# Expert tiles: SiLU on the gate half alone, the place read after the transpositions, TensorE's tile loop written out

## The chip, the core and the metric

The kernel runs on one core of a Trainium2 chip. Each of the core's engines follows its own instruction stream and meets the others through semaphores: TensorE (PE, with its weight loads shown apart as PEld), VectorE (DVE), ScalarE (ACT), GpSimd (POOL), and SyncE (SP), which issues DMAs. The metric is the device time of one execution in microseconds (us), lower is better. An engine's sequencer is the part that reads its instructions, computes addresses in registers, waits for semaphores and hands work on to the engine; in the profile its own instructions carry a q (PEldq for TensorE's).

## The reference, cut to what matters

Two transformer layers run one after the other on 4096 tokens of 256 channels; the change touches only the last block, a mixture of experts with a shared expert beside it:

```python
def _L1_ffn_ref(x, Wr, Wg, Wu, Wd, Sg, Su, Sd):      # 8 experts, hidden size 512
    xt = x.reshape(T, H)                              # T = 4096, H = 256
    scores = softmax(xt @ Wr)
    topk_w, topk_idx = top_k(scores, 2)
    topk_w = topk_w / (topk_w.sum(-1, keepdims=True) + EPS)
    g = silu(einsum('th,ehd->etd', xt, Wg))
    u = einsum('th,ehd->etd', xt, Wu)
    out_all = einsum('etd,edh->eth', g * u, Wd)
    out = sum(out_all[topk_idx, tok] * topk_w[..., None], axis=1)
    return out + silu(x @ Sg) * (x @ Su) @ Sd
```

## The kernel before

After routing, the tokens are sorted by expert and cut into NE = 71 tiles of 128 rows. Tile i is worked off by five engines at once, each with its own function of the same name `tile`, and what sets the order is the order in which each engine's code is written, with semaphores between them.

On TensorE, `tile(i, h)` does four things in this order. First `h_transpose_e(i - 1, ...)` transposes the hidden rows `hb` of the tile before (4 matmuls with the identity, L2260). Then `gate_up_e(i, ...)` multiplies the tile's tokens with the expert's gate matrix into PSUM bank 2 (w = 0) and its up matrix into bank 3 (w = 1): each product of 32-bit numbers is three matmuls of high and low parts (L1857 to L1859, the helper `three`), so 6 matmuls for the gate half and 6 for the up half. Then `x_transpose_e(i + 1, ...)` transposes the next tile's tokens (2 matmuls, L2244), and `down_e(i - 1, ...)` multiplies the transposed hidden rows of the tile before with the down matrix (12 matmuls, again L1857 to L1859, with `heh` and `hel` as operands).

Where an expert's weights lie in SBUF is known only at run time. `place_of(i)` (L2272) reads one number from the table `of_tile` in SBUF into a register of TensorE's sequencer and computes expert and address from it:

```python
def place_of(i):
    return pe.value_load(of_tile[0:1, bass.ds(i, 1)], min_val=0, max_val=SLOTS * E - 1)
```

In a looped pair of tiles the first one reads two places, its own and that of the tile before; the second one gets the latter from the first as a register and reads one. Tiles 0 to 4 and 67 to 70 are written out; tiles 5 to 66 run in `pe.Fori(2, (NE - 5) // 2)`, 31 turns of two tiles (L2312).

The other engines, per tile: ACT turns the transposed hidden rows into their high part `heh` (`h_high_e`, L789), then `silu_e(i)` computes SiLU of bank 2 into `gs` (L784), then `x_high_e(i + 1)` makes `xeh` (L779) and issues the load of a later tile's tokens. DVE makes the low part `hel` (`h_low_e`, L1798), then `hidden_e(i)` multiplies bank 3 with `gs` into `hb` (L1794), then `x_low_e(i + 1)` makes `xel` (L1788), then `y_out(i - 1)` copies the output to `ye` (L1806). SP stores `ye`. POOL gathers tokens, loads the experts' weights and splits them into high and low parts.

The semaphores that matter: `e_gu` (gate and up of a tile done), `e_si` (SiLU done), `e_hb` (hidden rows done), `e_ht` (transposed), `e_hlo` (`hel` done), `e_xlo` (`xel` done), `e_dn` (down done), `w_ready` (an expert's weights split). The transposition waits for `e_hb` of the tile before, and `gate_up_e` for `e_xlo`, `w_ready` and the same `e_hb`.

Of the kernel before, what the change touches and what calls it, by code (L numbers as in the profile page):

```python
# [40 lines left out]
E = 8  # L41
EH = 512
EW = 2 * KD * EH + EH // P * D
SLOT = 2 * EW
NE = 2 * NT + E - 1
# [22 lines left out]
def wait(eng, sem, n):  # L68

    if not isinstance(n, int) or n > 0:  # L70
        eng.wait_ge(sem, n)
# [22 lines left out]
def build(nc, cst, xT, x, wqkvgT, wave_cols, bias_cols, coupling_rows, woutT, bout, wgu_rows, wd_rows, wqk_T, wo_rows, bo, wr, experts, out):  # L94
    ctx = ExitStack()
    with ctx:
# [311 lines left out]
        def _(act):  # L408
# [366 lines left out]

            def x_high_e(i, h):
                act.wait_ge(e_t, i + 1)
                wait(act, e_gu, i - 1)
                act.activation(xeh[:, h].rearrange("p a c -> p (a c)"), PS[:, h, 0:D], ACT.Copy).then_inc(e_xhi, 1)  # L779

            def silu_e(i, h):
                act.wait_ge(e_gu, i + 1)
                wait(act, e_hb, i - 1)
                act.activation(gs[:, h], PS[:, 2], ACT.Silu).then_inc(e_si, 1)  # L784

# [9 lines left out]
            def tile(i, h, groups=None, first=False, final=False):  # L795
                if not first:
                    h_high_e(i - 1, 1 - h)
                silu_e(i, h)
                if not final:
                    x_high_e(i + 1, 1 - h)  # L800
                    if not isinstance(i, int) or DIRECT <= i + 3 < NE:
                        if groups is not None:
                            act.wait_ge(d_rows, 16 * groups)
                        rows(i + 3, 1 - h)

            x_high_e(0, 0)
            tile(0, 0, first=True)
            for i in range(1, 5):
# [18 lines left out]
            at = 4 * (NCH - 1) + 2  # L827
# [249 lines left out]
        def _(dve):  # L1077
# [62 lines left out]
            for cos_, _, turns in TABLES:  # L1140
                dve.tensor_scalar(cos_[:].bitcast(U32), turns[:].bitcast(U32), 0x7FFFFFFF, None, ALU.bitwise_and).then_inc(turns_done, 1)
# [647 lines left out]
                                  xeh[:, h].rearrange("p a c -> p (a c)").bitcast(F32), ALU.subtract).then_inc(e_xlo, 1)  # L1789

            def hidden_e(i, h):
                dve.wait_ge(e_si, i + 1)
                wait(dve, e_ht, i - 1)
                dve.tensor_tensor(hb[:, h], PS[:, 3], gs[:, h], ALU.mult).then_inc(e_hb, 1)  # L1794
# [13 lines left out]
            def tile(i, h, first=False, final=False):  # L1808
                if not first:
                    h_low_e(i - 1, 1 - h)  # L1810
                hidden_e(i, h)
                if not final:
                    x_low_e(i + 1, 1 - h)
                if not first:
                    y_out(i - 1, 1 - h)
# [34 lines left out]
            at = 4 * last + 3  # L1850
# [3 lines left out]
        def _(pe):  # L1854
            def three(out_, wh, wl, vh, vl, first, last_):

                pe.matmul(out_, wh, vh, start=first, stop=False)  # L1857
                pe.matmul(out_, wh, vl, start=False, stop=False)  # L1858
                return pe.matmul(out_, wl, vh, start=False, stop=last_)  # L1859
# [375 lines left out]
            def x_transpose_e(i, h):  # L2235
                rows = xe[:, h]
                if isinstance(i, int) and i < DIRECT:
                    pe.wait_ge((d_row0, d_row1)[h], 16 * (i // 2 + 1))
                    rows = xe[:, i] if i < 2 else xd[:, i - 2]
                else:  # L2240
                    pe.wait_ge(d_xe[h], 8 * (i - h) - 8 * (DIRECT - 2))
                wait(pe, e_xlo, i - 1)
                for k in range(KD):
                    t = pe.transpose(PS[:, h, k * P:(k + 1) * P], rows[:, k * P:(k + 1) * P], ident)  # L2244
                t.then_inc(e_t, 1)

            def gate_up_e(i, h, base_):
                pe.wait_ge(e_xlo, i + 1)
                wait(pe, e_hb, i)
                for w in range(2):  # L2250
                    for k in range(KD):
                        at, lo = (bass.ds(base_ + i * EW + (w * KD + k) * EH, EH) for i in range(2))
                        mm = three(PS[:, 2 + w], xeh[:, h, k], xel[:, h, k], EWs[:, at], EWs[:, lo], k == 0, k == KD - 1)
                mm.then_inc(e_gu, 1)

            def h_transpose_e(i, h):
                pe.wait_ge(e_hb, i + 1)
                wait(pe, e_hlo, i - 1)
                for j in range(4):
                    t = pe.transpose(PS[:, 4 + h, j * P:(j + 1) * P], hb[:, h, j * P:(j + 1) * P], ident)  # L2260
                t.then_inc(e_ht, 1)

            def down_e(i, h, base_):
                pe.wait_ge(e_hlo, i + 1)
                wait(pe, e_y, i - 1)
                for j in range(4):
                    at, lo = (bass.ds(base_ + i * EW + 2 * KD * EH + j * D, D) for i in range(2))
                    mm = three(PS[:, 6 + h, 0:D], heh[:, h, j], hel[:, h, j], EWs[:, at], EWs[:, lo], j == 0, j == 3)
                mm.then_inc(e_dn, 1)

            def place_of(i):
                return pe.value_load(of_tile[0:1, bass.ds(i, 1)], min_val=0, max_val=SLOTS * E - 1)  # L2272

            def tile(i, h, before=None, first=False, final=False):
                place = place_of(i)
                expert, at = place % E, place // E * SLOT
                if not first:
                    if before is None:
                        before = place_of(i - 1)
                        before = before // E * SLOT  # L2280
                    h_transpose_e(i - 1, 1 - h)
                pe.wait_ge(w_ready, expert + 1)
                gate_up_e(i, h, at)
                if not final:
                    x_transpose_e(i + 1, 1 - h)
                if not first:
                    down_e(i - 1, 1 - h, before)
                return at

# [14 lines left out]
            x_transpose_e(0, 0)  # L2304
            down_wide(1, 3)
            at = tile(0, 0, first=True)
            pe.wait_ge(d_add, 2 * AHEAD)
            at = tile(1, 1, at)
            at = tile(2, 0, at)
            at = tile(3, 1, at)  # L2310
            tile(4, 0, at)
            with pe.Fori(2, (NE - 5) // 2) as r:  # L2312
                at = tile(2 * r + 1, 1)
                tile(2 * r + 2, 0, at)
            at = tile(NE - 4, 1)
            for i in range(NE - 3, NE):
                at = tile(i, i % 2, at, final=i == NE - 1)
            h_transpose_e(NE - 1, 0)
            pe.wait_ge(d_xlo, AHEAD + 1)
# [92 lines left out]
```

## Time and profile before

| what | us |
|---|---|
| median of 3 runs | 1096.64 (1096.44 to 1098.18) |
| the profiled execution's own time | 1101.61 |
| its span, first to last instruction | 1099.7 |
| PE busy | 1032.2 (94%) |
| DVE busy | 764.7 (70%) |
| ACT busy | 489.6 (45%) |
| POOL busy | 442.0 (40%) |

The profiled execution took 1.91 us more than its span, and 4.97 us more than the median. Starts are in us from the span's start. A group of instructions has a line, an engine, an operation, what it writes and reads, a count, its busy time and the mean of one in ns; a bracket behind a timeline row tells how long the engine was idle before it and what ended that. "issue" means that the engine waited for nothing that the profile shows, so for its own sequencer or for something unseen. The experts' tiles lie between 611 and 982 us.

### The profile page before, as it was taken

What the parts mean: (1) busy time and instruction counts of PE and PEld (TensorE: products, weight loads), DVE (VectorE), ACT (ScalarE), POOL (GpSimd) and SP (SyncE); (2) the same over time, 40 slices, a digit from 0 to 9 for tenths busy, and PEclk for the clock granted to TensorE, in tenths of its full rate; (3) what the DMA queues carried; (4) which work ended last, traced back from release to release, by engine and by line L of the source; (5) the groups of instructions that cost most, each with busy time, mean ns of one, the idle gap of its engine ahead of it and who ended that gap; (6) DMA issues with size and microseconds to landing.
All of it is one profiled execution on the core that took longest, in us unless ns stands there. A gap on an engine that the chain in (4) does not pass through costs nothing.

```text
span 1099.7 us, 19315 instructions
## 1 busy us (share of the span) xinstructions
PE 1032.2 (94%) x5960; PEld 901.9 (82%) x5961; DVE 764.7 (70%) x1290; ACT 489.6 (45%) x914; POOL 442.0 (40%) x445
## 2 busy tenths in 40 slices
PE   6898997799999999999999999989999999999994
PEld 5676776799999998999988787878888888888883
DVE  7988998899999987787878343333444444347886
ACT  6745755774344444666751222222322222233326
POOL 1000201555544446322100787975633200018886
PEclk9999998999999999999999999999999999999997
DMA  8100000010000000311250557464413111213335
GB/s 315 70 32 20 1 29 1 1 35 1 0 0 0 0 1 1 120 40 39 64 205 6 187 172 242 141 183 160 156 52 107 56 48 54 70 58 108 123 106 191
DMA packets 41350, 87.83 MB, mean 80 GB/s; under 512 B 5970, under 2 KB 27732, under 8 KB 39892
## 3 DMA queue, kind: packets, MB, share of 16 engines
q0 software_dynamic: 9696, 35.66, 10.5%
q1 hardware_dynamic: 20804, 39.20, 10.0%
q10 hardware_dynamic: 10800, 12.32, 3.6%
q8 instruction: 29, 0.48, 0.2%
q14 instruction: 21, 0.17, 0.0%
HBM read 57.80 MB, written 29.36 MB: 79 GB/s over the span
## 4 chain that ended last, share of the span: by engine, by line
PE 53%; DVE 19%; DVEq 10%; POOL 8%; issue 5%; ACT 4%; DMA 1%; ACTq 0%; POOLq 0%
PE PS L1857 14%; PE PS L1859 13%; PE PS L1858 13%; POOL gathered L1043 6%; PE PS L2260 3%; PE PS L2012 2%; DVEq L1433 2%; DVEq L1280 2%; POOL pause L1047 1%; DVEq L1447 1%; PE PS L2244 1%; DVE hx L1292 1%; PE PS L1910 1%; DVEq L1293 1%; DVE qinv L1283 1%
## 5 line engine op out<-in xcount | busy, mean ns | idle before, releaser
L1794 DVE TENSOR_TENSOR hb<-PS,gs 128x512 f32<-128x512 f32 x71 | 49.1, 692 | 154.0 <-ACT gs L784 143.4
L1043 POOL DMA_INDIRECT gathered<-expert_outputs,pos x64 | 66.7, 1043 | 139.5 <-DMA expert_outputs<-ye 127.2
L1857 PE MATMUL PS<-EWs,xeh 128*128 x284 | 119.8, 422 | 0.0
L784 ACT ACTIVATE gs<-PS 128x512 f32<-128x512 f32 x71 | 42.5, 598 | 162.3 <-PE PS L1859 154.0
L1859 PE MATMUL PS<-EWs,xel 128*128 x284 | 112.5, 396 | 0.0
L1858 PE MATMUL PS<-EWs,xeh 128*128 x284 | 111.8, 394 | 0.0
L1857 PE MATMUL PS<-WGh,bxh 128*128 128x352 f32 x256 | 88.0, 344 | 13.4 <-DVE hv L1427 10.5
L2012 PE MATMUL PS<-WD,htf 128*128 128x256 f32 x384 | 88.5, 380 | 1.6 <-ACT htf L573 1.5
L1857 PE MATMUL PS<-EWs,heh 128*128 x284 | 85.7, 302 | 3.9 <-issue 3.9
L789 ACT ACTIVATE heh<-PS 128x512 fp32r<-128x512 f32 x71 | 42.5, 598 | 104.4 <-PE PS L2260 86.9
L1798 DVE TENSOR_TENSOR hel<-PS,heh 128x512 fp32r<-128x512 f32 x71 | 49.1, 691 | 55.0 <-ACT heh L789 46.3
L1858 PE MATMUL PS<-WGl,bxh 128*128 128x352 f32 x256 | 85.3, 333 | 0.0
L1859 PE MATMUL PS<-WGh,bxl 128*128 128x352 f32 x256 | 85.2, 333 | 0.0
L2012 PEld LDWEIGHTS PS<-WD,htf 128*128 128x128 f32 x384 | 71.2, 190 | 10.9 <-ACT htf L573 2.5
L1858 PE MATMUL PS<-EWs,heh 128*128 x284 | 80.1, 282 | 0.0
L1859 PE MATMUL PS<-EWs,hel 128*128 x284 | 80.0, 282 | 0.0
L865 POOL TENSOR_TENSOR bq<-bx,qsc 128x512 f32<-128x512 f32 x16 | 19.6, 1226 | 117.9 <-DVE bx L1294 117.9
L1857 PEld LDWEIGHTS PS<-EWs,xeh 128*128 128x128 f32 x284 | 53.9, 190 | 16.0 <-issue 0.6
L1857 PEld LDWEIGHTS PS<-WGh,bxh 128*128 128x128 f32 x256 | 50.2, 196 | 17.2 <-issue 11.9
L1859 PEld LDWEIGHTS PS<-EWs,xel 128*128 128x128 f32 x284 | 53.7, 189 | 10.5
L1858 PEld LDWEIGHTS PS<-EWs,xeh 128*128 128x128 f32 x284 | 53.9, 190 | 9.4
L1857 PEld LDWEIGHTS PS<-EWs,heh 128*128 128x128 f32 x284 | 53.5, 188 | 4.7 <-issue 4.6
(387 smaller groups left out, 3013.5 us busy)
## 6 DMA issues: line engine op xcount, KB each, us to landing
raw_of<-experts POOLq DMA_DIRECT2D x6, 1536.0 KB
expert_outputs<-ye SPq DMA_DIRECT2D x71, 128.0 KB
xe<-tokens_by_expert ACTq DMA_DIRECT2D x65, 128.0 KB
xraw<-xT SPq DMA_DIRECT2D x8, 512.0 KB, 4.1
X<-x SPq DMA_DIRECT2D x1, 4096.0 KB, 13.3
tokens<-X SPq DMA_DIRECT2D x8, 512.0 KB, 3.1
y<-X SPq DMA_DIRECT2D x7, 512.0 KB
raw_of<-experts SPq DMA_DIRECT2D x2, 1536.0 KB, 9.5
```

The source lines that it names most:

```text
L784: act.activation(gs[:, h], PS[:, 2], ACT.Silu).then_inc(e_si, 1)
L789: act.activation(heh[:, h].rearrange("p a c -> p (a c)"), PS[:, 4 + h], ACT.Copy).then_inc(e_hhi, 1)
L1043: pool.indirect_dma_start(out=gathered[c][:, j, t], out_offset=None, in_=YS, in_offset=bass.IndirectOffsetOnAxis(ap=pos[:, j, 4 * c + t:4 ...
L1280: dve.drain()
L1433: dve.drain()
L1794: dve.tensor_tensor(hb[:, h], PS[:, 3], gs[:, h], ALU.mult).then_inc(e_hb, 1)
L1798: dve.tensor_tensor(hel[:, h].rearrange("p a c -> p (a c)"), PS[:, 4 + h], heh[:, h].rearrange("p a c -> p (a c)").bitcast(F32), ALU.subtr ...
L1857: pe.matmul(out_, wh, vh, start=first, stop=False)
L1858: pe.matmul(out_, wh, vl, start=False, stop=False)
L1859: return pe.matmul(out_, wl, vh, start=False, stop=last_)
L2012: mm = pe.matmul(PS[:, 7, i * D:(i + 1) * D], htf[:, i, k], WD[:, k], start=k == 0, stop=k == FT - 1)
L2260: t = pe.transpose(PS[:, 4 + h, j * P:(j + 1) * P], hb[:, h, j * P:(j + 1) * P], ident)
```

## The change

Three edits. (1) TensorE signals `e_gu` after the gate half and again after the up half. ACT's SiLU waits for the first of the two signals, and DVE's product now waits itself for the second one as well as for the SiLU. (2) In TensorE's `tile`, the transposition comes first and the read of the place follows it. (3) TensorE's loop is gone: tiles 5 to 66 are written out, and each passes its place on to the next, so every tile reads one. The loops of ACT, DVE and SP stay.

```diff
             def x_high_e(i, h):
                 act.wait_ge(e_t, i + 1)
-                wait(act, e_gu, i - 1)
+                wait(act, e_gu, 2 * i - 2)
...
             def silu_e(i, h):
-                act.wait_ge(e_gu, i + 1)
+                act.wait_ge(e_gu, 2 * i + 1)
                 wait(act, e_hb, i - 1)
...
             def hidden_e(i, h):
+                dve.wait_ge(e_gu, 2 * i + 2)
                 dve.wait_ge(e_si, i + 1)
...
                         mm = three(PS[:, 2 + w], xeh[:, h, k], xel[:, h, k], EWs[:, at], EWs[:, lo], k == 0, k == KD - 1)
-                mm.then_inc(e_gu, 1)
+                    mm.then_inc(e_gu, 1)
...
             def tile(i, h, before=None, first=False, final=False):
+                if not first:
+                    h_transpose_e(i - 1, 1 - h)
                 place = place_of(i)
                 expert, at = place % E, place // E * SLOT
-                if not first:
-                    if before is None:
-                        before = place_of(i - 1)
-                        before = before // E * SLOT
-                    h_transpose_e(i - 1, 1 - h)
                 pe.wait_ge(w_ready, expert + 1)
                 gate_up_e(i, h, at)
                 if not final:
                     x_transpose_e(i + 1, 1 - h)
                 if not first:
+                    if before is None:
+                        before = place_of(i - 1)
+                        before = before // E * SLOT
                     down_e(i - 1, 1 - h, before)
                 return at
...
-            tile(4, 0, at)
-            with pe.Fori(2, (NE - 5) // 2) as r:
-                at = tile(2 * r + 1, 1)
-                tile(2 * r + 2, 0, at)
-            at = tile(NE - 4, 1)
-            for i in range(NE - 3, NE):
+            at = tile(4, 0, at)
+            for i in range(5, NE):
                 at = tile(i, i % 2, at, final=i == NE - 1)
```

On TensorE, this is where one looped turn begins in the kernel before. `hb` are the hidden rows, `of_tile` the table of places; "ISA" and "REGISTER_ALU" are the sequencer's own steps, and the matmul at L2260 is the first of the transpositions:

```order
L2272 TENSOR_LOAD of_tile
L2272 ISA x3
L2272 TENSOR_LOAD of_tile
L2272 ISA x2
L71 REGISTER_ALU [waits d_ehb]
L2260 MATMUL PS<-C,hb 128x128 [waits d_ehlo]
L2260 MATMUL PS<-C,hb 128x128 x3
L2282 ISA
L2248 REGISTER_ALU [waits d_wready]
L1857 ISA [waits d_ehb,d_exlo]
L1857 MATMUL PS<-EWs,xeh 128x512
```

And this is the same place, between two tiles, in the changed kernel, whose lines from L1794 on count one more:

```order
L1860 MATMUL PS<-EWs,hel 128x256
L2261 MATMUL PS<-C,hb 128x128 [waits d_ehlo,d_ehb]
L2261 MATMUL PS<-C,hb 128x128 x3
L2273 TENSOR_LOAD of_tile
L2273 ISA x2
L2280 ISA
L1858 ISA [waits d_ehb,d_exlo,d_wready]
L1858 MATMUL PS<-EWs,xeh 128x512
```

Both reads stood ahead of the transposition and its wait for `e_hb`; now one read stands between the transposition and the first gate matmul.

On DVE, around the product `hb` of a looped tile, `hel`, `xel` and `ye` being the low parts and the output copy, the kernel before has:

```order
L1798 TENSOR_TENSOR hel<-PS,heh 128x512 [waits d_ehhi]
L1794 TENSOR_TENSOR hb<-PS,gs 128x512 [waits d_eht,d_esi]
L1787 REGISTER_ALU
L1788 TENSOR_TENSOR xel<-PS,xeh 128x256 [waits d_exhi]
L1806 COPY ye<-PS 128x256 [waits d_est1,d_edn]
```

and the changed kernel:

```order
L1799 TENSOR_TENSOR hel<-PS,heh 128x512 [waits d_ehhi]
L1792 ISA
L1795 TENSOR_TENSOR hb<-PS,gs 128x512 [waits d_eht,d_esi,d_egu]
L1787 REGISTER_ALU
L1788 TENSOR_TENSOR xel<-PS,xeh 128x256 [waits d_exhi]
L1807 COPY ye<-PS 128x256 [waits d_est1,d_edn]
```

The order of DVE's work is the same; the product has one wait more and one register step ahead of it.

## Rows read from the trace of the kernel before

**Rows 1.** The page, busy time and share of the span.

```profile
PE 1032.2 (94%) x5960; PEld 901.9 (82%) x5961; DVE 764.7 (70%) x1290; ACT 489.6 (45%) x914; POOL 442.0 (40%) x445
```

**Rows 2.** Busy time by stretch: start:end, us, engines (count), clock, DMA share, GB/s.

```profile
632.00:742.00 110.00, 102.47 (x587) 86.74 (x587) 42.71 (x80) 29.09 (x60) 90.59 (x93) 0.97 0.62 185
742.00:953.00 211.00, 211.00 (x1253) 181.72 (x1252) 88.18 (x166) 61.20 (x125) 57.14 (x15) 1.00 0.27 89
953.00:978.00 25.00, 25.00 (x152) 21.79 (x151) 11.79 (x23) 8.03 (x15) 0.00 (x0) 1.00 0.13 42
```

**Rows 3.** Timeline of PE: start, us; transpositions of tiles 5, 25, 67 and last.

```profile
633.03 0.65 PE L2260 MATMUL PS<-C,hb 128*128 128x128 f32 x4
...
745.87 0.65 PE L2260 MATMUL PS<-C,hb 128*128 128x128 f32 x4
...
958.06 0.60 PE L2260 MATMUL PS<-C,hb 128*128 128x128 f32 x4
...
977.88 0.66 PE L2260 MATMUL PS<-C,hb 128*128 128x128 f32 x4
```

**Rows 4.** Timeline of one written-out tile, from its first gate matmul.

```profile
968.46 0.49 PE L1857 MATMUL PS<-EWs,xeh 128*128 x1
968.80 0.39 PE L1858 MATMUL PS<-EWs,xeh 128*128 x1
...
969.72 0.39 PE L1859 MATMUL PS<-EWs,xel 128*128 x1
...
971.09 0.39 PE L1859 MATMUL PS<-EWs,xel 128*128 x1
...
971.52 0.60 ACT L784 ACTIVATE gs<-PS 128x512 f32<-128x512 f32 x1 [2.27 <-PE PS L1859]
...
972.14 0.69 DVE L1794 TENSOR_TENSOR hb<-PS,gs 128x512 f32<-128x512 f32 x1 [1.78 <-ACT gs L784]
...
972.75 0.41 DVE L1788 TENSOR_TENSOR xel<-PS,xeh 128x256 fp32r<-128x256 f32 x1
972.84 0.28 PE L1859 MATMUL PS<-EWs,hel 128*128 x1
972.96 0.60 PE L2260 MATMUL PS<-C,hb 128*128 128x128 f32 x4
...
973.42 0.49 PE L1857 MATMUL PS<-EWs,xeh 128*128 x1
```

**Rows 5.** Sequencer's steps by line: ns min/median/max, first and last start.

```profile
L2272 PEldq TENSOR_LOAD <-of_tile x1: 300/300/300, 971.4 to 971.4; - x1
...
L2272 PEldq SEQ_ASSERT  x1: 18/18/18, 972.0 to 972.0; - x1
L2282 PEldq FUSED_REGOPS  x1: 76/76/76, 972.9 to 972.9; - x1
L2312 PEldq COMPARE_BRANCH  x21: 222/222/222, 743.4 to 946.1; - x21
```

**Rows 6.** The same for the reads of 684 to 686.8 and of 632 to 742.

```profile
L2272 PEldq TENSOR_LOAD <-of_tile x2: 299/602/904, 684.5 to 685.9; - x2
...
L2272 PEldq TENSOR_LOAD <-of_tile x29: 297/305/918, 632.2 to 738.5; - x29
```

**Rows 7.** Timeline, and who PE waited for (us, times, longest).

```profile
686.63 0.65 PE L2260 MATMUL PS<-C,hb 128*128 128x128 f32 x4 [1.88 <-issue]
...
735.91 0.60 ACT L789 ACTIVATE heh<-PS 128x512 fp32r<-128x512 f32 x1 [5.75 <-remote]
...
737.43 0.38 PE L1857 MATMUL PS<-EWs,heh 128*128 x1 [2.92 <-issue]
...
PE PS L2260 <- issue: 4.5, 6, 1.9
```

**Rows 8.** Instruction fetches in 440 to 600 and 600 to 980: packets, MB, share.

```profile
q8 instruction: 9, 0.15, 0.4%
...
q8 instruction: 4, 0.07, 0.1%
```

## The prediction

> **What bounds the kernel now.** The page first: PE is busy 94% of the span and no other engine over 70% [rows 1], so what counts is what PE does and what delays it. Then the stretches [rows 2]: from 742 to 953 us PE's busy time is the whole 211.00 of 211.00. Busy does not mean at its peak, since PE's durations overlap, so the third view is the pace: the starts of the transpositions. Tiles 25 to 67 took (958.06 - 745.87) / 42 = 5.05 us each, and these are looped tiles; the four written out behind the loop took (977.88 - 958.06) / 4 = 4.955 us each [rows 3]. Same matmuls, 0.1 us less. Tiles 5 to 25 took (745.87 - 633.03) / 20 = 5.64 us each [rows 3]; there the DMAs are at 0.62 against 0.27, the clock at a mean of 0.97 and PE busy only 102.47 of 110 us [rows 2].
>
> The fourth view is one written-out tile [rows 4]. Call the start of its first gate matmul G = 968.46. The last gate matmul starts at G + 1.26 (969.72), the last up matmul at G + 2.63, SiLU at G + 3.06, the product `hb` at G + 3.68, and `hb` ends at G + 4.37. The last down matmul starts at G + 4.38, the transposition at G + 4.50 and the next gate matmul at G + 4.96. So two chains end together: PE's own queue, and last up matmul, SiLU, `hb`, transposition. A third is just behind: `xel` waits on DVE for `hb` and ends at G + 4.70, and the next gate matmul needs it. And the second gate matmul comes 0.34 us after the first, where the others stand (971.09 - 968.80) / 10 = 0.229 us apart: TensorE's sequencer is 0.1 us late there.
>
> Fifth, the sequencer. Its read begins at 971.4 and is done at 972.0 [rows 5], while PE still works on the matmuls queued before; then nothing happens in the sequencer until `hb` is done (972.14 + 0.69 = 972.83), and its next step (L2282) starts at 972.9 [rows 4, 5]. So a wait for a semaphore stops the sequencer, while matmuls already handed on run.
>
> **The change part by part.** *The loop goes.* A turn has a branch (0.22 us, rows 5) and a second read (0.6 us with its register steps, rows 5) ahead of the first tile's transposition. Most of it hides behind the queue, but the measured difference between a looped and a written-out tile is 5.052 - 4.955 = 0.097 us. For 62 looped tiles: 6.0 us.
>
> *The early SiLU.* It can start at G + 1.26 + 0.43 = G + 1.69, if PE's last matmul and ACT's start stand as far apart as now (971.09 to 971.52, rows 4), and ends at G + 2.29. Then `hb` waits for the up half alone: G + 2.63 + 0.43 = G + 3.06, plus the additional wait in DVE's sequencer. No row shows that; the nearest steps, 18 to 76 ns each [rows 5], bound it by 0 and 0.15, and I take 0.08. So `hb` runs from G + 3.14 to G + 3.83, 0.54 us earlier, and `xel` ends well before it is needed. Alone this would bring nearly nothing at the transposition, since PE's own queue holds it at G + 4.50; what it frees is the sequencer, at about G + 3.89.
>
> *The read behind the transposition.* From there the sequencer hands on the transpositions, reads the place (0.6 + 0.05 us) and needs what it needs now from the transposition's release to the first gate matmul: 972.9 to 973.42, 0.52 us, of which some 0.1 is the wait for `xel` (ends 973.16), which goes. That gives G + 3.89 + 0.65 + 0.42 = G + 4.96. The bounds are 0.1 us below (no additional wait in DVE, 4.88) and 0.1 us above (the wait for `xel` was not what took the time, 5.05). PE's own work gives 0.46 + 12 x 0.229 + 0.23 + 12 x 0.117 = 4.84 if the sequencer is never late, and 4.95 with its lateness. So I take 4.95 us a tile: the room that the early SiLU makes (0.54 us) is used up by the read (0.65 us) that is moved into it, and the written-out pace of now remains. Queued behind the moved read on TensorE are the expert's wait (`w_ready`) and all of gate and up; nobody else waits for it. SP's and POOL's queues are passed by nothing.
>
> *The DMA-heavy stretch.* 20 tiles at 5.05 would be 101.0 us; they took 112.84 [rows 3], so 11.8 us are irregular. One kind is at the loop's turns: PE waited 4.5 us in 6 pieces just ahead of a transposition for nothing that the profile shows, the longest 1.88 us at 686.63 [rows 7]. In that piece stand both reads of a turn, one of them taking 904 ns instead of 300 [rows 6]. The mean clock of 0.97 over 110 us [rows 2] is 0.03 x 110 / 0.5 = 6.6 us at the lower level of 1.2 GHz; it fell after the two longest idle times of PE, this one and the next, so each cost half of 3.3 us, some 1.6 us, beside itself. So reads explain about 6.1 us. The other kind is at 734 to 746: `heh` waited 5.75 us for a signal of work that PE had long done, and PE then 2.92 us [rows 7]; with the half clock behind it this one cost some 4.7 us. The profiled execution is 4.97 us above the median, so I take this to be of that execution alone; that is argued, not shown. The rest, 1.0 us, I leave.
>
> With the change a turn's second read is gone, but each read is now where nothing covers it: a slow one costs up to 0.6 us in full. Of 29 reads from 632 to 742 the median is 305 ns and the longest 918 [rows 6]; I allow 2.1 us (five of 20 reads slow by 0.4 us).
>
> *Instruction fetch.* Written out, TensorE's stream is longer. In 440 to 600 us, where PE's code has no loop, the queue q8, TensorE's by its rest while TensorE loops, fetched 9 times, once per 17.8 us, and the share of 0.4% of 16 engines in 160 us is about 1.1 us each; from 600 to 980 it was 4 [rows 8]. So about 325 / 17.8 = 18 fetches come in. PE was not left waiting for any of the nine, so I cost them at nothing; their cover is the code already fetched, and without it they cost 18 x 1.1 = 20 us.
>
> Here a rule of the Trainium skill bears on the case. The page Runtime: NRT & Kernel Launch, section Instruction fetch mechanics, says that a taken branch whose target is outside the window of fetched code forces a fetch and stalls. By that rule 31 turns would each hold a fetch, and writing out would bring far more than 6 us. The trace does not agree that it happens here: the branch took 222 ns in all 21 turns from 743 to 946 and fetches were only 4 in 380 us [rows 5, 8]; the sum goes without it.
>
> **The sum.** In the profiled execution tiles 5 to 67 took 325.0 us [rows 3]. After: 62 x 4.95 = 306.9, plus 2.1 = 309.0. Against its own time: 1101.6 - 16.0 = 1085.6. Against the median, which I take to be without the 4.7 us: 320.3 - 309.0 = 11.3, so 1096.6 - 11.3 = 1085.3. What comes behind the tiles (the shared expert on PE, the gather on POOL) starts from their end and moves with it. POOL isn't late: it is busy 57 of 211 us [rows 2].
>
> **The rivals.**
>
> 1. *The sequencer gets ahead.* If the next step after the wait is quicker than I count, the pace is PE's own work, 4.85: another 6.2 us, 1079. For it: PE's own sum. Against it: the read is longer than the room made for it. A gain in the irregular part beyond mine, up to 4.7 us, would land there too.
> 2. *The read stands in the way.* If the whole 0.52 us stays behind the read and DVE's additional wait costs 0.15, the pace is 5.05 to 5.1, as in the loop; then only the irregular part brings something: 320.3 - 313.1 - 2.1 = 5.1, so 1091.5; at 5.1 us, 1094.6. This is also the case in which the change doesn't do what it says, the reads being no better hidden than before.
> 3. *Slower: fetches.* If code can't be fetched in time under the heavy DMAs or in general, 18 fetches at 1.1 us give 20 us against 11.3 gained: 1105. It decides from 0.63 us of PE's idle time per fetch on. Against it: the nine fetches that cost nothing, at a DMA load lower than that of 632 to 742, though.
> 4. *About the same: slow reads.* Were 15 of the 20 reads in the DMA-heavy stretch slow by 0.6 us and the pace 5.05, the change brings 320.3 - 313.1 - 9.0 = -1.8 us, nothing that can be told: 1098. Before, the median read there was a quick one [rows 6].
>
> **How the numbers follow.** Forecast 1085 (0.58, from 1082 to 1089); rival 1, 1079 (0.15); rival 2, 1092 (0.17); rival 4, 1098 (0.05); rival 3, 1105 (0.05). Rival 2's outermost end, 0.02 of its 0.17, lies within 0.2% too. The range from 1078 to 1094 leaves out rivals 3 and 4 and the outer ends of 1 and 2. The bound of 0.2% is 2.2 us, about what a measurement of this kernel can tell from no change: faster 0.88, the same 0.07, slower 0.05.
>
> **What the profile of the changed kernel would show.** The transpositions at 4.95 us from tile 25 on. SiLU starting before the last up matmul, some 0.4 us behind the last gate matmul, and `hb` 0.5 us behind the last up matmul. The transposition 0.12 us behind the last down matmul everywhere. The first gate matmul 0.45 us behind the transposition: if it is 0.55 or more, the read is in the way (rival 2); the second 0.23 instead of 0.34 us behind the first would be rival 1. No clock loss around 686. About 18 more fetches in q8, and no idle time of PE in line with them. The forecast is wrong if TensorE's sequencer can't pass on the transposition before PE has finished the down matmuls: then the read starts only at G + 4.5, the pace is near 5.5, and the time would be above 1110.

## The result and the profile after

The changed kernel takes 1087.88 us (median of 6 runs, 1086.42 to 1091.55) against 1096.66 before: a ratio of 0.9921, 95% interval 0.9904 to 0.9937, so 8.8 us less. The forecast was 1085, with a range of 1078 to 1094. Its profiled execution took 1091.20 us, 10.4 less than that of before.

The pace first, as in [rows 3]: the transpositions of tiles 5, 24, 25, 26, 67 and the last one, from PE's timeline of the changed kernel.

```profile
633.28 0.60 PE L2261 MATMUL PS<-C,hb 128*128 128x128 f32 x4
...
729.62 0.60 PE L2261 MATMUL PS<-C,hb 128*128 128x128 f32 x4
738.09 0.93 PE L2261 MATMUL PS<-C,hb 128*128 128x128 f32 x4 [1.94 <-DVE hb L1795]
744.86 0.60 PE L2261 MATMUL PS<-C,hb 128*128 128x128 f32 x4
...
948.28 0.60 PE L2261 MATMUL PS<-C,hb 128*128 128x128 f32 x4
...
967.53 0.60 PE L2261 MATMUL PS<-C,hb 128*128 128x128 f32 x4
```

Tiles 5 to 67 take 315.0 us instead of 325.0. From tile 26 on the pace, the mean interval between two transpositions, is (948.28 - 744.86) / 41 = 4.96 us, forecast 4.95. Tiles 5 to 25 take 104.8 us instead of 112.8: 8.0 of the 10 us come from the DMA-heavy stretch. The busy times by stretch, as in [rows 2], say the same: in 632 to 742 us PE now works 105.44 us and not 102.47.

```profile
632.00:742.00 110.00, 105.44 (x624) 90.74 (x623) 45.65 (x84) 32.48 (x62) 90.64 (x93) 0.98 0.62 189
742.00:943.00 201.00, 201.00 (x1218) 175.48 (x1218) 88.45 (x162) 64.17 (x122) 57.29 (x15) 1.00 0.28 93
```

Next, two tiles in a row, as in [rows 4], again from the timeline. A tile's first gate matmul stands at 809.95, its last gate matmul at 811.20 and its last up matmul at 812.56; the next tile's first at 814.95 and last at 817.57.

```profile
809.95 0.49 PE L1858 MATMUL PS<-EWs,xeh 128*128 x1
...
811.20 0.39 PE L1860 MATMUL PS<-EWs,xel 128*128 x1
...
811.63 0.60 ACT L784 ACTIVATE gs<-PS 128x512 f32<-128x512 f32 x1 [0.84 <-PE PS L1860]
...
812.56 0.39 PE L1860 MATMUL PS<-EWs,xel 128*128 x1
...
813.15 0.69 DVE L1795 TENSOR_TENSOR hb<-PS,gs 128x512 f32<-128x512 f32 x1 [1.63 <-PE PS L1860]
...
814.43 0.60 PE L2261 MATMUL PS<-C,hb 128*128 128x128 f32 x4
...
814.95 0.50 PE L1858 MATMUL PS<-EWs,xeh 128*128 x1
...
817.57 0.39 PE L1860 MATMUL PS<-EWs,xel 128*128 x1
...
818.00 0.69 DVE L1795 TENSOR_TENSOR hb<-PS,gs 128x512 f32<-128x512 f32 x1 [1.61 <-PE PS L1860]
...
819.44 0.60 PE L2261 MATMUL PS<-C,hb 128*128 128x128 f32 x4
...
819.86 0.50 PE L1858 MATMUL PS<-EWs,xeh 128*128 x1
```

SiLU starts 0.43 us behind the last gate matmul, as worked out, and what ends DVE's wait is now PE. But `hb` starts 0.59 us behind the last up matmul in one tile and 0.43 in the other. In the first one DVE's sequencer runs two steps of its own at 813.0 and 813.1, between the end of the last up matmul (812.95) and the product:

```profile
L1793 DVEq ALU_OP  x1: 40/40/40, 813.0 to 813.0; - x1
L71 DVEq EVENT_SEMAPHORE  x1: 21/21/21, 813.1 to 813.1; - x1
```

In the second one it has none there: the product itself waits for `e_gu`. Some 0.1 of the 0.16 us travel on: transposition to gate matmul takes 0.52 us in the first and 0.42 in the second. The reads of the two places, from TensorE's sequencer:

```profile
L2273 PEldq TENSOR_LOAD <-of_tile x1: 308/308/308, 813.9 to 813.9; - x1
...
L2273 PEldq TENSOR_LOAD <-of_tile x1: 299/299/299, 818.7 to 818.7; - x1
```

`hb` ends at 813.84 and 818.69, and the reads begin right there, 0.5 and 0.7 us before TensorE's array runs the transpositions (814.43 and 819.44). So the sequencer is stopped by the semaphore and not by the array, and the read is on the path from `hb` to the next gate matmul.

### The profile page after: what moved, and what is told of

Read it like the earlier page. It is cut to its first block, busy times and chain, and to the rows that moved or that the text cites. A ratio compares the mean times of both kernels' runs of the same rounds, so it can differ in the third digit from the quotient of the medians.

```text
span 1089.3 us, 19081 instructions
## 1 busy us (share of the span) xinstructions
PE 1022.1 (94%) x5960; PEld 895.6 (82%) x5960; DVE 768.2 (71%) x1290; ACT 496.4 (46%) x914; POOL 441.0 (40%) x445
## 4 chain that ended last, share of the span: by engine, by line
PE 50%; DVE 21%; DVEq 11%; POOL 6%; issue 5%; ACT 5%; DMA 1%; another core or an unknown queue 0%; ACTq 0%
PE PS L1858 14%; PE PS L1859 13%; PE PS L1860 13%; POOL gathered L1043 5%; PE PS L2261 3%; PE PS L2013 2%; DVEq L1280 2%; DVEq L1433 2%; DVEq L1447 2%; DVE hx L1292 1%; PE PS L2245 1%; POOL pause L1047 1%; ACT X L756 1%; DVEq L1293 1%; DVE qinv L1283 1%
## 5 line engine op out<-in xcount | busy, mean ns | idle before, releaser
L1858 PEld LDWEIGHTS PS<-EWs,xeh 128*128 128x128 f32 x284 | 53.6, 189 | 19.3 <-issue 6.7
L779 ACT ACTIVATE xeh<-PS 128x256 fp32r<-128x256 f32 x71 | 27.2, 384 | 85.4 <-PE PS L2245 81.3
L1807 DVE COPY ye<-PS 128x256 f32<-128x256 f32 x71 | 30.2, 425 | 48.0 <-PE PS L1860 41.1
```

The costliest lines, as they stand in the source:

```text
L1807: dve.tensor_copy(ye[:, h], PS[:, 6 + h, 0:D]).then_inc(e_y, 1)
```

## The experiments

The lines of the experiments' kernels are those of before or a few further on. A time is the median of 4 to 6 executions where nothing else is said, a ratio is against the kernel before beside it. Paces are those of tiles 26 to 67, and where an average of a step within the tile is given, it is over these tiles.

**1. The loop alone.** Only the last hunk of the diff.

```diff
-            tile(4, 0, at)
-            with pe.Fori(2, (NE - 5) // 2) as r:
-                at = tile(2 * r + 1, 1)
-                tile(2 * r + 2, 0, at)
-            at = tile(NE - 4, 1)
-            for i in range(NE - 3, NE):
+            at = tile(4, 0, at)
+            for i in range(5, NE):
```

> Only TensorE's loop is written out; the one read of each tile stays ahead of the transposition, and SiLU still waits for both halves. Sequencer theory: the pace of tiles 25 to 67 becomes that of today's written-out tiles, 4.95 us against 5.05, and the idle pieces at the loop's turns in the DMA-heavy stretch go, since a single read, even a slow one, is covered by the queued down matmuls: 1086 to 1089. Rival (the gain came from the early SiLU): pace 5.05 and not under 1094.

Measured: 1088.91 us, a ratio of 0.9924 (0.9907 to 0.9941). The changed kernel has 0.9921. Taking away the loop alone brings what the whole change brings, and the other two edits together bring nothing that can be told. Its pace is (945.85 - 742.00) / 41 = 4.97 us; PE's timeline has the transpositions of tiles 25, 26 and 67.

```profile
736.99 0.65 PE L2260 MATMUL PS<-C,hb 128*128 128x128 f32 x4 [0.45 <-issue]
742.00 0.66 PE L2260 MATMUL PS<-C,hb 128*128 128x128 f32 x4
...
945.85 0.60 PE L2260 MATMUL PS<-C,hb 128*128 128x128 f32 x4
```

**2. The early SiLU alone**, in the looped kernel.

```diff
-                wait(act, e_gu, i - 1)
+                wait(act, e_gu, 2 * i - 2)
...
-                act.wait_ge(e_gu, i + 1)
+                act.wait_ge(e_gu, 2 * i + 1)
...
+                dve.wait_ge(e_gu, 2 * i + 2)
...
-                mm.then_inc(e_gu, 1)
+                    mm.then_inc(e_gu, 1)
```

> Only SiLU begins on the gate half; the loop stays, with two reads, one read, two reads ahead of the transpositions. Sequencer theory: the second tile of a turn gets to some 4.85 us, the first one stays at 5.0 to 5.05 because its two reads still end last; together 4.93 to 4.95, and the idle pieces at the turns stay: 1089 to 1092. Rival (hidden rows were never what was late, only the loop): 1096.

Measured: 1095.54 us (10 runs), 0.9985 (0.9973 to 0.9998). That is less gain than I expected, and nearly what the rival said. PE's timeline, with the last down matmul ahead of each transposition and the gate matmul behind it, first for the tile that opens a turn, then for the second one:

```profile
802.38 0.28 PE L1860 MATMUL PS<-EWs,hel 128*128 x1
802.72 0.65 PE L2261 MATMUL PS<-C,hb 128*128 128x128 f32 x4
803.24 0.49 PE L1858 MATMUL PS<-EWs,xeh 128*128 x1
...
807.64 0.28 PE L1860 MATMUL PS<-EWs,hel 128*128 x1
807.76 0.60 PE L2261 MATMUL PS<-C,hb 128*128 128x128 f32 x4
808.12 0.48 PE L1858 MATMUL PS<-EWs,xeh 128*128 x1
```

The second tile gains: 0.12 and then 0.36 us. In the first one the transposition stands 0.34 us behind the last down matmul, since the two reads don't come any earlier than before: they begin at 801.2 and 802.0, the first of them 1.5 us ahead of the transposition, as it is in the kernel before (805.0 for a transposition at 806.54). The pace is 5.03, and tiles 5 to 25 take 111.2 us: what the early SiLU gains is lost to the two reads of the next turn.

**3. The read behind the transposition without the early SiLU**, loop gone.

```diff
+                if not first:
+                    h_transpose_e(i - 1, 1 - h)
                 place = place_of(i)
                 expert, at = place % E, place // E * SLOT
-                if not first:
-                    if before is None:
-                        before = place_of(i - 1)
-                        before = before // E * SLOT
-                    h_transpose_e(i - 1, 1 - h)
```

> The loop is written out and the read stands behind the transposition, but SiLU waits for both halves as before. Sequencer theory: the wait for the hidden rows stops the sequencer until 4.45 us after the first gate matmul, then the read (0.65) and the rest (0.42 to 0.52) follow: a pace of 5.5 to 5.6 us and a time of 1120 to 1128. Rival (the sequencer passes the waiting transposition on and reads meanwhile): 4.95 us and 1088.

Measured: 1125.77 us, 1.0248 (1.0223 to 1.0274), a pace of 5.50 us. Timeline, and the read in the sequencer:

```profile
802.32 0.69 DVE L1794 TENSOR_TENSOR hb<-PS,gs 128x512 f32<-128x512 f32 x1 [2.74 <-ACT gs L784]
...
803.13 0.60 PE L2260 MATMUL PS<-C,hb 128*128 128x128 f32 x4
```

```profile
L2272 PEldq TENSOR_LOAD <-of_tile x1: 297/297/297, 803.1 to 803.1; - x1
```

`hb` ends at 803.01, and only then the read begins. This is the disputed cost by itself: 5.50 - 4.97 = 0.53 us a tile against experiment 1, nearly the read's 0.6. The rival, that the sequencer passes the waiting transposition on and reads meanwhile, is out. The first transposition that waits has three more behind it, ahead of the read, so no run tells at which of the four the sequencer stops.

**4. Loop gone and early SiLU, the read left ahead of the transposition.** The hunks of experiments 1 and 2.

> The loop is written out and SiLU begins on the gate half, but the read stays ahead of the transposition. Sequencer theory: the read is covered by queued matmuls, the wait for the hidden rows ends at 3.9 us behind the first gate matmul, so the sequencer is half a microsecond ahead at the next gate half, and PE's own work alone sets the pace: 4.85 us, so 6 to 7 us below the changed kernel, 1080 to 1083. Rival (PE's own pace is 4.95, the 0.34 us between the first two gate matmuls being the array's): the same as the changed kernel, 1087 to 1089.

Measured: 1080.09 us, 0.9845 (0.9824 to 0.9866), and once more, beside experiment 8:

> The kernel with the loop gone, the early SiLU and the read ahead of the transposition once more, on the same chip as the run beside it, for the comparison: 1079 to 1083, with its hold-up of some 5 us near 730.

1079.14 us, 0.9830 (0.9812 to 0.9847). The pace is 4.84 us both times; the interval of tile 26 still belongs to the hold-up described below, and from tile 27 on it is 4.82. This version beats both kernels, the one before by 18 us and the changed one by some 8. Between transposition and gate matmul there are now 0.36 us:

```profile
812.29 0.60 PE L2261 MATMUL PS<-C,hb 128*128 128x128 f32 x4
...
812.65 0.48 PE L1858 MATMUL PS<-EWs,xeh 128*128 x1
...
812.97 0.39 PE L1859 MATMUL PS<-EWs,xeh 128*128 x1
```

Of the 0.14 us a tile against the changed kernel 0.10 are in that place (0.47 there on average). The step from the first to the second gate matmul is still 0.32 us. As the wait for `hb` is over well before in this kernel, I take it that a late sequencer doesn't make that step; what does is not shown.

**5. Early SiLU and read behind, but looped.** The changed kernel with the loop of before.

> The early SiLU and the read behind the transposition, but TensorE's loop stays; the first tile of a turn reads the place of the tile before between the token transposition and down. Sequencer theory: the second read and the branch are now covered by queued matmuls, so a turn costs little: pace 4.95 to 5.05 and 1088 to 1094. Rival (the loop itself costs 0.1 us a tile whatever stands where): pace 5.05 to 5.1, 1094 to 1098.

Measured: 1103.28 us, 1.0051 (1.0034 to 1.0068), a pace of 5.21 us; both expectations were too low. Transposition to gate matmul takes 0.71 us on average, where the changed kernel has 0.47. In the loop the read's address and the waits need register steps of their own (as in the first of the two pieces of order shown with the change), and behind the transposition they are on the path. In one tile of this kernel, in which `hb` ends at 815.93, the sequencer shows:

```profile
L71 PEldq ALU_OP  x1: 36/36/36, 816.0 to 816.0; - x1
L2273 PEldq FUSED_REGOPS  x1: 42/42/42, 816.1 to 816.1; - x1
...
L2273 PEldq TENSOR_LOAD <-of_tile x1: 302/302/302, 816.2 to 816.2; - x1
```

So the read begins 0.2 to 0.3 us behind the end of `hb`, where the changed kernel's begins at once; a further step of 32 ns stands behind the read, at 817.0. That accounts for most of the 0.24 us. So edit 2 costs more in a loop than written out: by the ratios, taking the loop away is worth some 14 us with edits 1 and 2 in both, and with neither 8 to 9.

**The hold-up near 730 us.** It comes before experiments 6 to 8, because every kernel so far has it. In the changed one, around 732 us:

```profile
732.33 0.42 DVE L1807 COPY ye<-PS 128x256 f32<-128x256 f32 x1 [2.83 <-remote]
...
733.00 0.60 ACT L789 ACTIVATE heh<-PS 128x512 fp32r<-128x512 f32 x1 [3.96 <-remote]
...
735.86 0.60 ACT L784 ACTIVATE gs<-PS 128x512 f32<-128x512 f32 x1 [2.26 <-remote]
```

The same as in [rows 7]: DVE and ACT wait for signals of matmuls that PE had finished long before ("remote": no instruction ended when the signal came). In experiment 3, where PE is two tiles behind by then, the long interval (7.3 us) starts with tile 22 and not 24, but at 729.7 us as well. It keeps to the time and not to the tile, which points at another engine's work. And at 723 to 740 us POOL issues its last 11 gathers of token rows with no piece of weight splitting in between.

**6. The changed kernel with these gathers spaced**, by five small GpSimd additions (1.3 us together) behind each of them.

```diff
                         fetch(stages[g % STAGES][:, n], i, d_stage[g % 2])
+                        if g >= 14:
+                            for turn in range(5):
+                                spacing.append(0)
+                                pool.tensor_tensor(freed[:, 2:4], zrow[:, 0:2], zrow[:, 0:2], ALU.add).then_inc(spaced, 1)
+                                pool.wait_ge(spaced, len(spacing))
...
```

> The changed kernel with some 1.3 us of small GpSimd operations after each of the last 11 gathers of token rows, those that follow each other without a piece of weight splitting between them (723 to 740 us in the trace). Theory that these close gathers hold back TensorE's signals: no interval between transpositions over 5.4 us from 725 to 745, where the changed kernel has 8.47 and 6.77. Rival (it belongs to the execution or to something else at that time): the long intervals stay near 730. The total is no measure here, since expert 4 is loaded 15 us later and TensorE has to wait for it near 770: 1090 to 1100.

Measured: 1100.69 us (one run). Its transpositions from 724 to 746 us:

```profile
724.95 0.60 PE L2267 MATMUL PS<-C,hb 128*128 128x128 f32 x4
730.27 0.60 PE L2267 MATMUL PS<-C,hb 128*128 128x128 f32 x4
735.29 0.60 PE L2267 MATMUL PS<-C,hb 128*128 128x128 f32 x4
740.14 0.60 PE L2267 MATMUL PS<-C,hb 128*128 128x128 f32 x4
745.14 0.60 PE L2267 MATMUL PS<-C,hb 128*128 128x128 f32 x4
```

No interval here is over 5.32 us, where the changed kernel has 8.47 and 6.77. The time itself is lost again at tile 32, which waits for expert 4's weights, loaded later: one interval of 18.9 us at 770.

**7. Experiment 4's kernel with expert 4 loaded before the last gathers**, without and with the spacing.

```diff
-            gather_tokens(14, len(GROUPS))
             load_expert(4)
+            gather_tokens(14, len(GROUPS))
```

> The kernel with the loop gone, the early SiLU and the read ahead of the transposition, and expert 4's weights fetched before the last 11 gathers instead of behind them. Both theories: the hold-up near 730 stays or grows, since more is moved at the time; expert 4 wasn't late: 1079 to 1084.

> As the run before, and the last 11 gathers are spaced by 1.3 us each. Close gathers theory: the hold-up near 730 (5 us) goes, 1074 to 1077. Rival: it stays, 1079 to 1084.

The first is inconclusive: its four executions scatter from 1081.48 to 1113.14 us. Its profile, of an execution of 1099.81 us, has the hold-up, 8.11 us between two transpositions at 726.6. Tiles 5 to 67 took 305.0 us in it and 305.7 in experiment 4's, so what that execution lost, it lost behind the experts' tiles. The second took 1089.57 us: the hold-up is gone (no interval over 5.04 us between 675 and 763), but expert 4 is split after the spaced gathers, and its first tile waits: 17.0 us at 763. So the expectation for the time was missed, and that on the hold-up met. This run also settles a rival, that the mere amount of DMA traffic holds the signals back. From 725 to 730 us, with expert 4's weights coming in, the DMA engines were at 0.98 and moved 378 GB/s, more than the 253 GB/s or less of the changed kernel from 725 to 740, and PE lost nothing. The row, as in [rows 2]:

```profile
725.00:730.00 5.00, 5.00 (x33) 4.46 (x32) 2.51 (x5) 1.58 (x3) 3.79 (x13) 1.00 0.98 378
```

**8. The gathers spaced by useful work**: expert 4 loaded before the last two groups of expert 3's splitting, and split in pieces between the last gathers.

```diff
-            gather_tokens(12, 14, split=3, part=8)
-            gather_tokens(14, len(GROUPS))
             load_expert(4)
+            gather_tokens(12, 14, split=3, part=8)
+            pool.wait_ge(d_raw2, 16 * 3)
+            gather_tokens(14, len(GROUPS), split=4, every_=1)
+            split_part(4, PARTS - 1)
             keep(len(GROUPS) - 1)
-            loaded(4)
```

> Loop gone, early SiLU, read ahead of the transposition, and the last 11 gathers are spaced by useful work: expert 4 is loaded some 16 us earlier and split in pieces between them. Close gathers theory: no interval over 5.4 us from 720 to 745, and expert 4 is ready 20 us before its first tile (32, near 765 us): 1074 to 1077. Rival (spacing gives back elsewhere what it frees, or the load beside the gathers holds up PE as much): 1079 to 1084.

Measured: 1076.03 us, 0.9802 (0.9785 to 0.9819), against 1079.14 for experiment 4's kernel beside it on the same chip. It is the fastest of all. Its timeline:

```profile
719.37 0.60 PE L2262 MATMUL PS<-C,hb 128*128 128x128 f32 x4
...
721.00 0.50 PE L1859 MATMUL PS<-EWs,xeh 128*128 x1 [1.03 <-POOL EWs L978]
...
725.49 0.60 PE L2262 MATMUL PS<-C,hb 128*128 128x128 f32 x4
...
730.31 0.60 PE L2262 MATMUL PS<-C,hb 128*128 128x128 f32 x4
...
735.13 0.60 PE L2262 MATMUL PS<-C,hb 128*128 128x128 f32 x4
```

From 725 on the interval is 4.82 us. One of 6.12 remains before it, against my expectation, and it is another thing: tile 23 is the first of expert 3, and POOL finishes splitting its weights only then. Of the 5 us of the hold-up 3.1 were gained. At this one tile POOL is now the limit: the splitting ends at 720.80 here and at 720.51 in experiment 4, where the tile's first gate matmul comes at 720.62, just behind it.

## Why the prediction was right, point by point

*The two chains that end together* was right. Experiments 3 and 4 differ from the changed kernel in one edit each and experiment 1 in two, and they give 5.50, 4.84 and 4.97 us where it has 4.96.

*The loop, 6.0 us from the pace*, was right in kind and a little too large: 4.97 and 4.96 for 5.05, so some 5 us over 62 tiles. The larger part came from where the forecast had it too: most of the idle pieces at the loop's turns are gone [rows 7]. With the loop alone taken away (experiment 1) PE's waits for "issue" ahead of a transposition are 1.1 us in 3 pieces instead of 4.5 in 6. In the changed kernel there are none; PE waits for "issue" ahead of the gate or down matmuls instead, in short pieces that stand at slow reads and in the hold-up. Among the tiles the lower clock of 1.2 GHz appears only in and behind the hold-up, where the mean clock is 0.84; before it and behind it the clock is 1.00, around 686 us too. The row, as in [rows 2]:

```profile
734.00:745.00 11.00, 8.45 (x44) 7.02 (x45) 3.48 (x7) 2.56 (x5) 6.13 (x8) 0.84 0.81 187
```

PE's waits in the changed kernel from 600 to 980 us (us, times, longest):

```profile
PE PS L1858 <- issue: 3.9, 7, 1.1
...
PE PS L2261 <- DVE hb L1795: 2.6, 2, 1.9
```

*The room of the early SiLU used up by the read* was right, and is the main thing to learn from this case. The room came to 0.46 or 0.62 us instead of 0.54, as the additional wait in DVE cost 0.16 us in one tile of two and nothing in the other: these are the two bounds that I had given, and their mean is the value taken.

*The second gate matmul 0.1 us late by the sequencer* was wrong. It comes 0.32 to 0.34 us behind the first in every kernel. The 0.1 us that PE could gain lie between transposition and gate matmul (0.46 in the written-out tile before, 0.36 in experiment 4). The sum of PE's own work, 4.84, came within 0.02 us of experiment 4's 4.82 by luck: it has the first step 0.1 us too long and the second one 0.1 us too short. So rival 1 named the wrong place for its proof.

*The hold-up as one of that execution* was wrong. It is in all profiles without spaced gathers, and costs 8.47 + 6.77 - 2 x 4.96 = 5.3 us here. The prediction had 4.7 for the kernel before; counted in the same way as here it is 5.0 there (8.76 and 6.36 us against 5.05). As it is in both kernels it hardly moved the difference, but the step from the profiled execution's 4.97 us above the median to this cause failed: the changed kernel's profiled execution is 3.3 us above its own median with the hold-up, and experiment 4's is at its median (1080.09) with it.

*Slow reads, 2.1 us*: tiles 5 to 24 took 96.3 us where 19 times 4.96 make 94.2, so 2.1. Four of its 20 reads there took 588 to 885 ns, and they stand at tiles 6, 11, 14 and 15, whose intervals are the long ones: 5.59, 5.20, 5.47 and 5.44 us, together 1.9 us over the pace. In experiment 4 a read is covered again, though not wholly: one of 887 ns goes with an interval of 4.86 us, one of 912 with one of 5.41. Tiles 5 to 25 take 99.2 us there against 104.8, of which 19 x 0.14 = 2.7 are the pace and 2.6 that the hold-up's first interval is shorter (5.89 instead of 8.47).

*The sum.* For tiles 5 to 67 with the hold-up kept, it gives 306.9 + 2.1 + 4.7 = 313.7 us; measured 315.0. The missing 1.3 us are the pace (0.01 us in each of 62 tiles, 0.6) and the larger hold-up (0.6). The medians differ by 8.8 us where 11.3 were forecast, and the upper end of the interval is 10.5; part of this gap is that before's profiled execution, on which the sum rests, was further above its median than that of after.

*Instruction fetches* cost nothing, as forecast: from 600 to 980 us there are 24, 20 more than in [rows 8], and PE waited for none.

```profile
q8 instruction: 24, 0.39, 0.4%
```

Here the Trainium skill's page Runtime: NRT & Kernel Launch, section Instruction fetch mechanics, calls the crossing of a block mostly hidden; the trace agrees, with PE at 201.00 of 201 us from 742 to 943. That branches were costly by a fetch, as the same section warns of branches out of the fetched window, was not what the loop cost here: its turns have a second read of 0.6 us and a branch of 0.22, sometimes with a slow read between them. The prediction went too far when it had each of the 31 turns hold a fetch by that rule, since nothing showed that the turns left the window.

## What to carry to other kernels

A register read on an engine's sequencer belongs ahead of the wait that stops it, where queued matmuls cover it, and not behind it; moving it behind the wait needs as much room as the read takes, and an edit that makes the room then only pays for the move. Edits that are made together should be costed alone: here one of three carried the whole gain, one was worth some 9 us once the loop was gone, and the third took them back. When an engine waits for a signal whose sender had long been done, look for what keeps to the same time in kernels of different pace.

## What the runs showed of the hardware

A wait of TensorE's matmuls for a semaphore stops its sequencer until the signal comes (`hb` ended at 803.01 us in experiment 3, and the read behind the four transpositions began at 803.1); once it has come, the sequencer goes on while the matmul still stands in the queue: in the changed kernel a read began at 813.9 us and the transpositions ahead of it ran at 814.43. A read of one number from SBUF takes 0.30 us, 0.6 with its register steps, and in the DMA-heavy stretch up to 0.9 (1.35 in experiment 3). Close software gathers on GpSimd (one per 1.25 us, 11 with nothing but writes of whole groups of rows between them) go along with signals of TensorE that arrive some 3 to 4.5 us behind the end of the matmul: `heh` started at 733.00 us for transpositions that ended at 730.22, and at 735.91 for 731.40 in the kernel before. With 1.3 us of other work between the gathers this was gone in three kernels of three. How they act on the signals stays open. The amount of traffic alone it is not (378 GB/s without a loss in experiment 7); whether it is the number of descriptors or something in GpSimd's own code was not told apart.
